# A drain of TensorE's queue raises the count of finished quads in a four-layer graph network

## The reference, cut to what matters

```
cnt  = segment_sum(ones, dst * 10 + relation)          # count pass
sums = segment_sum((h @ w_rel)[src], seg)              # gather by source, add by destination
mean = sums / max(cnt, 1)                              # relational layers, two of them
h    = segment_sum(hr[type, src] * norm, dst)          # typed layer
agg  = segment_sum(h[src], dst) / deg                  # SAGE layers, two of them
Wij  = (ssp(f_ij @ W1 + b1) @ W2 + b2) * rcut          # filter of the last block
agg  = segment_sum(h[idx_j] * Wij, idx_i)              # last block: its roles are swapped in the kernel's scatter
```

## Time and profile before

| | us |
|---|---|
| median of 3 runs | 19062.55 |
| lowest and highest | 19050.81, 19082.07 |
| profiled execution, its own time | 19022.15 |
| its span | 19020.4 |
| PE busy in the span | 8494.8 (45%) |
| DVE busy | 7085.7 (37%) |
| POOL busy | 10847.9 (57%) |

### The profile page before, as it was taken

How to read it: one execution, slowest core, us unless ns; L and a number is a source line. 1 busy time by engine, 2 the same in 40 slices (tenths; PEclk the granted TensorE clock), 3 DMA queues, 4 the chain that set the end, 5 groups by cost and what they waited for, 6 DMA issues and landing times.

```text
span 19020.4 us, 184637 instructions
## 1 busy us (share of the span) xinstructions
PE 8494.8 (45%) x37745; PEld 6761.0 (36%) x37746; DVE 7085.7 (37%) x33940; ACT 2444.3 (13%) x4374; POOL 10847.9 (57%) x10307
## 2 busy tenths in 40 slices
PE   2453333336333334333343333333333377777777
PEld 1233333333233333232232222332222255555555
DVE  7644444443222223222222222235555534444443
ACT  0120000002000001000010000000000034444443
POOL 0034444443666664666646666656666628888883
PEclk9975555558555556555565555555555557777775
DMA  2131111113111113111121111123333236666665
GB/s 82 68 112 34 33 33 33 33 34 151 44 45 45 45 45 98 45 45 45 44 63 45 44 44 44 45 70 82 82 83 84 82 78 118 118 117 118 117 118 122
DMA packets 981255, 1326.88 MB, mean 70 GB/s; under 512 B 201421, under 2 KB 635620, under 8 KB 981180
## 3 DMA queue, kind: packets, MB, share of 16 engines
q0 software_dynamic: 552016, 851.84, 20.2%
q1 hardware_dynamic: 429208, 474.72, 8.5%
HBM read 992.21 MB, written 333.54 MB: 70 GB/s over the span
## 4 chain that ended last, share of the span: by engine, by line
another core or an unknown queue 30%; DVE 20%; issue 18%; DMA 10%; PE 9%; POOL 7%; DVEq 2%; ACT 2%; POOLq 0%; ACTq 0%; SPq 0%
DMA agg_dram<-acc,sum_row 8%; DVE tab_s L1127 6%; POOL agg_dram L582 4%; PE ps L745 3%; DVE xn_h L1135 2%; POOL scratch L597 2%; DVE tab_s L1087 2%; PE ps L911 2%; DVE xn_h L1142 1%; DVE acc L1017 1%; PE ps L869 1%; POOL rows L597 1%; DVE tab_s L1056 1%; DVE xs L1066 1%
## 5 line engine op out<-in xcount | busy, mean ns | idle before, releaser
L597 POOL DMA_INDIRECT scratch<-table_dram,row_st x4160 | 3998.8, 961 | 2729.7 <-issue 1265.4
L597 POOL DMA_INDIRECT rows<-table_dram,row_st x4160 | 3997.0, 961 | 2532.1 <-issue 1932.1
L745 PE MATMUL ps<-tab_s,rows 128*128 128x128 f32 x8320 | 2105.2, 435 | 3527.5 <-DMA rows<-table_dram,row_st 2211.1
L745 PE MATMUL ps<-tab_s,scratch 128*128 128x128 f32 x8320 | 2093.7, 433 | 3451.4 <-DMA scratch<-table_dram,row_st 2395.2
L745 PEld LDWEIGHTS ps<-tab_s,rows 128*128 128x128 f32 x8320 | 1842.2, 326 | 3776.0 <-issue 3769.0
L745 PEld LDWEIGHTS ps<-tab_s,scratch 128*128 128x128 f32 x8320 | 1832.3, 325 | 3694.3 <-issue 3565.4
L582 POOL DMA_INDIRECT agg_dram<-acc,sum_row x1664 | 2649.1, 1592 | 529.0 <-issue 379.7
L1017 DVE TENSOR_TENSOR acc<-ps,acc 128x128 f32 x2080 | 606.4, 292 | 5977.3 <-remote 3909.8
L1127 DVE TENSOR_SCALAR tab_s<-iota,rw_st 128x128 f32<-128x128 f32 x6656 | 1909.6, 361 | 238.3 <-issue 236.8
L745 PE MATMUL ps<-scratch,tab_s 128*128 128x128 f32 x3328 | 667.2, 365 | 836.4 <-DVE scratch L1234 801.0
L1066 DVE CUSTOM_DVE_ANT_0 xs<-ps,tab_s 128x128 f32<-128x128 f32 x1664 | 384.5, 288 | 1468.7 <-remote 1293.5
(11 more groups left out here) (189 smaller groups left out, 11966.0 us busy)
## 6 DMA issues: line engine op xcount, KB each, us to landing
scratch<-in_src_row SPq DMA_DIRECT2D x832, 256.0 KB
table_dram<-tab_s POOLq DMA_DIRECT2D x200, 640.0 KB, 3.2
scratch<-in_dst_row SPq DMA_DIRECT2D x416, 256.0 KB
rows<-table_dram,row_st POOLq DMA_INDIRECT x4160
scratch<-table_dram,row_st POOLq DMA_INDIRECT x4160
scratch<-table_dram SPq DMA_DIRECT2D x416, 64.0 KB
agg_dram<-acc,sum_row POOLq DMA_INDIRECT x1664
scratch<-agg_dram SPq DMA_DIRECT2D x100, 256.0 KB, 3.8
```

Source lines behind the costliest of these rows:

```text
L597: pool.indirect_dma_start(row_banks[bank][:, u, :], None, table_dram[p["rels"]], bass.IndirectOffsetOnAxis(ap=row_st[:, bank, u:u + 1], ax ...
L745: mm = pe.matmul(o, lhs[:, u, :], rhs[:, u, :], start=j == 0 or not summed, stop=j == QUAD - 1 or not summed)
```

## The change

In `quad_products` the semaphore update is taken off the quad's last product and is given to a drain, an instruction of TensorE's queue that stands right behind it. It holds the queue until the engine is empty. The function is used in all seven passes, so 2912 drains are added, and nothing else is touched.

```
@@ -744,7 +744,7 @@
                     o = ps[q][0:m, 0:P] if summed else ps[q][0:m, j * P:(j + 1) * P]
                     mm = pe.matmul(o, lhs[:, u, :], rhs[:, u, :], start=j == 0 or not summed,
                                    stop=j == QUAD - 1 or not summed)
-                mm.then_inc(mm_done, 1)
+                pe.drain().then_inc(mm_done, 1)
```

## The result

The changed kernel takes 19342.21 us (median of 4 runs, 19335.00 to 19356.53) against 19068.42 us (4 runs, 19050.81 to 19082.07) for the kernel before. The ratio is 1.0145, 95% interval 1.0127 to 1.0163: slower by 1.45%, clear of the spread, where I had forecast 18,130. The profiled execution took 19335.0 us. (A later experiment ran the same pair on another chip: 16305.07 us with the change, 16301.71 without.)

The account below looks back on a forecast made before the run. It took POOL's pauses behind late counts in the first three PLAIN passes as the bound. 19,022 - 1000 + 21 + 42 + 5 = 18,090, with 40 for the runs' median 18,130 us; 8-in-10 range 17,950 to 19,450.

Parts of the forecast that it names:

- Where POOL would stand with prompt counts: Gathers of the first three PLAIN passes: POOL's own rate is the next limit, 2093 us a pass, freeing 1052 us.
- A, B and C: The first three PLAIN passes, profiled at 2425, 2445 and 2461 us, where the whole gain was forecast.
- If the drain's count is prompt: Condition for the gain: DVE then adds within some 0.2 us of the product in the first three PLAIN passes.
- the 1000 us of gain: Gain taken in the first three PLAIN passes out of 1052 us, leaving some for pauses that remain.
- Its array was empty of them: Argument that a drain would not wait: PE went on with three quads while the count was late.
- the first rival: Drain waits for the same late event and holds PE's queue: 19,062 + 291 to 811, middle about 19,450; chance 0.22.
- Second rival: Count late by the same path, PE not held; only drains' cost left: 19,062 + 0 to 130; chance 0.17.
- Third: Lateness moves to DVE's `hot_ready` and `row_staged` once POOL does not pause; half the gain left, 18,600; chance 0.11.
- A drain's own cost: About 0.1 us where a quad's end is waited for: COUNT 21, LOOKUP 42, last PLAIN 5, FILTER 0 us.
- within 0.2%: Whole kernel: time within 38 us of no change, part of the second rival's case; chance 0.10.

Follow-up runs that it names:

- e3_both: Kernel before, with the last product still raising the count and a drain without a count behind it in all passes; 19323.38 us, ratio 1.0166.
- e1: Kernel before, with the drain raising the count only in the first three PLAIN passes; 19264.52 us, ratio 1.0137.
- e2: Kernel before, with drains raising the count in all passes except the first three PLAIN ones; 19043.43 us, ratio 1.0024.
- e6: Kernel before, without drain, but one of a quad's four products done in the first three PLAIN passes; 18738.11 us against 18947.57.
- h1: Kernel before, but one product a quad in the first three PLAIN passes, a drain behind it raising the count; 18749.04 us against 18987.28.
- i1_change: The change itself again, on a chip without late counts; 16305.07 us against 16301.71 for the kernel before, ratio 1.0002.
- h3_thin_drain: Kernel before, but in the first three PLAIN passes four products of 32 columns a quad, a drain raising the count; 16294.03 us against 16283.59.
- h4: Kernel before, but in the first three PLAIN passes two of four products a quad, a drain raising the count; 16329.08 us against 16283.59.

## Why the prediction was wrong

*Where POOL would stand with prompt counts.* Right in its size, within 2 us, though not by the drain: I had 2093 us a pass, and where counts are prompt A, B and C take 2092 or 2093 each. Together they are 1054 us below the lengths; I had summed 1052. The bound was read rightly; what the change does to it was not.

*"If the drain's count is prompt."* This is the step that failed, and with it the 1000 us of gain: A, B and C lost 329. The argument was that counts raised from a queue are prompt in the same passes. But a queue's count that follows a plain wait and one that follows a drain are two things: the drain first has to learn that the engine is done, and it learned this as late as the product's own count came (14.76 us of idle time behind the third quad in the timeline above; 20.8 at the longest of VectorE's waits, against 20.1 to 20.5 of the earlier trace rows). e3_both shows it from the other side: with the count back on the product, the drain alone costs as much.

*"Its array was empty of them."* My argument against the first rival. The quads that TensorE did during a late count (from 5533.53, 5538.39 and 5543.50 on, each after 2.8 to 3.3 us of idle time, when its rows had landed) show that it can go on with work, not that the chip takes the earlier work for complete. The Trainium skill (PSUM — Partial Sum Buffer, section "Engine vs sequencer instructions") has a drain wait until the engine is fully idle, and has the product's update fire on completion. Where counts are late, the trace agrees with the first half only if "idle" means reported idle, which here comes up to 20 us after the last product's record ends; the second half it contradicts by the same time, if a product is complete where its record ends. The profile models these ends, so the runs do not part a product that is done and told late from one that is done late. Where counts are prompt, both hold (add 0.24 us after the quad).

*The first rival's working.* Its mechanism, a held queue, is the one measured, with the wrong place. I let A, B and C go at about nothing, since TensorE could catch up before the next rows land. That is so (the quads from 5549.01 on follow each other at 0.32 to 0.41 us), but row numbers wait for the group's last quad, and this quad now stands behind the release: 2.37 us per pair of groups, 329 us measured in three passes (229 between e1 and e2). In the LOOKUP pass I had 291 to 520 us, and e2 against e1 gives 14; in the last PLAIN pass 0 to 291, and 17. Why LOOKUP loses so little was not tried. My sum was wrong too: 19,062 + 291 to 811 is 19,353 to 19,873, with its middle at 19,613 and not at 19,450, and the result lies 11 us below its lower end. That 19,450 came within 108 us of the result is luck: two errors of opposite sign in the passes, and one in the sum. For the same reason the top of my range, 19,450, covers less of this rival than the half that I gave it.

*Second rival* (late by the same path, nothing held, 0 to 130 us): out by the loss of 274 us and by e3_both. *Third* (lateness moves to VectorE once POOL does not pause): not seen after the change, where VectorE's waits are for PEq L747. Its mechanism is there when TensorE's counts cease to be late: with one product a quad, TensorE waits up to 11.2 us for `hot_ready`, and POOL still pauses some 270 us a pass (e6, h1).

*A drain's own cost.* COUNT: +21 forecast, +12 to 13 measured (0.03 us a drain), on both kinds of chip (the LOOKUP pass begins at 1152.4 in i1_change and at 1140.5 in h3_thin_drain, which has no drain in COUNT). Between quads whose inputs are there it leaves 0.32 us. LOOKUP: +42 forecast, +14. FILTER: 0 forecast, +2, hidden behind POOL.

*What I could not have read.* The trace before was of one execution on one chip. Nothing in it said that 1052 us of A, B and C, some 1140 of LOOKUP and 500 of the last PLAIN pass belong to the place or the time of the run. The outcome that I gave 0.10, "within 0.2%", is the one measured on the only chip without late counts on which the change itself ran.

## What to carry to other kernels

A drain is a wait. In every run here its count came as late as the product's own where that was late, and as promptly where it was prompt; it made no late count earlier, and while it waited no later product of its queue started. Before pricing a held queue, look at what the last item behind the hold feeds (here 16 row numbers and POOL's next burst), not only at whether the engine catches up. And a trace full of waits that nothing explains should be taken again on other chips before a kernel is tuned against it: here the same kernel lost 2,700 us to them on some and none on others.

## What the runs showed of the hardware

- On the chips of the first runs, during POOL's bursts of indirect gathers, the counts that TensorE's products raise came up to 20 us after the products' records ended (longest wait 20.8 us), and instructions of TensorE and VectorE with nothing to wait for had 0.9 to 1.8 us of idle time before them. With one product a quad VectorE's counts were the late ones instead (TensorE waited up to 11.2 us for them). Plain DMAs from the same queue had none of it (longest wait 2.9 us); a quarter of the bytes did not help (20.5 us).
- In the FILTER pass of the same traces, where POOL's indirect DMAs are scatters of 1.59 us each, no drain lasted over 3.95 us, against 21.8 in A, B and C and 28.8 in the LOOKUP pass.
- On three other chips, later, the kernel before took 16,284 to 16,302 us against 18,948 to 19,068, and in the traces taken there (the change, and the kernels of h3 and h4) no gathering pass has a pause of POOL beyond its 0.30 us between instructions.
- A drain behind a single product per quad lasted 0.69 to 0.77 us on a chip with late counts, behind four products 5.6 us in the mean. Number or length of the products: open. Why indirect DMAs do this, and only on some chips or at some times, is open too.
